# First attention: fp32 probabilities as the moving operand instead of a two-part fp16 split

## The reference, cut to what matters

```python
B, Sq, Sk, HEADS, hd = 2, 512, 1024, 16, 32       # x (2, 512, 512), ctx (2, 1024, 512)
scores = einsum('bhqd,bhkd->bhqk', qh, kh) / sqrt(hd)
causal = ki <= qi + (Sk - Sq)                      # the last 512 keys are causal
attn = softmax(where(causal, scores, -10000.0))
out = einsum('bhqk,bhkd->bhqd', attn, vh)          # keys and values are both ctx itself
```

## Time and profile before

| | us |
|---|---|
| median of 3 runs | 1868.09 (1862.59 to 1871.82) |
| span of the profiled execution, first to last instruction | 1858.6 |
| first attention in it | 234 to 571 |
| PE, DVE, ACT busy over the span | 1482.2, 1148.1, 933.8 |

### The profile page before, as it was taken

One profiled execution on the slowest core, in us unless ns is written; L12 is line 12 of the kernel. 1 busy time (PEld: TensorE's weight loads), 2 busy tenths in 40 slices (PEclk: granted clock), 3 DMA queues, 4 the chain that ended last, 5 costly groups with the idle time before them and its releaser, 6 DMA issues.

```text
span 1858.6 us, 30566 instructions
## 1 busy us (share of the span) xinstructions
PE 1482.2 (80%) x11006; PEld 830.7 (45%) x11064; DVE 1148.1 (62%) x2005; ACT 933.8 (50%) x1195; POOL 370.5 (20%) x179
## 2 busy tenths in 40 slices
PE   6885288888885299999999999277878787778777
PEld 3443155555554144444444444134545454444434
DVE  5888699899895211111111111569999999995565
ACT  3554388788783011111111111138998999892853
POOL 1101000000000366899940000320000000000150
PEclk9998599999997599999999999688999999999998
DMA  5567111121110699999988882640000000000101
GB/s 180 176 183 251 69 61 60 60 75 60 60 66 1 256 403 366 382 384 403 404 331 302 305 308 112 211 114 26 28 26 25 13 25 25 25 1 1 68 1 46
DMA packets 102757, 273.90 MB, mean 147 GB/s; under 512 B 7209, under 2 KB 11305, under 8 KB 101681
## 3 DMA queue, kind: packets, MB, share of 16 engines
q1 hardware_dynamic: 87904, 223.65, 32.4%
q0 software_dynamic: 10816, 40.90, 7.1%
q10 hardware_dynamic: 3984, 8.65, 1.2%
HBM read 212.62 MB, written 38.27 MB: 135 GB/s over the span
## 4 chain that ended last, share of the span: by engine, by line
PE 44%; DVE 34%; issue 11%; DMA 4%; ACT 3%; POOL 2%; SPq 1%; DVEq 1%; POOLq 0%; ACTq 0%
PE scores L859 17%; DVE arena L1615 15%; PE bank L875 9%; DVE arena L1420 6%; DVE arena L1434 3%; DMA arena<-in_ctx 2%; PE scores L686 2%; PE bank L773 2%; PE bank L1059 2%; PE bank L991 1%; PE bank L867 1%; DVE arena L1621 1%; PE bank L904 1%; PE bank L757 1%; PE scores L920 1%
## 5 line engine op out<-in xcount | busy, mean ns | idle before, releaser
L1615 DVE TENSOR_SCALAR_CACHE_REDUCE arena<-scores,arena 128x1024 f32<-128x1024 f32 x256 | 317.4, 1277 | 14.5 <-PE scores L920 14.3
L859 PE MATMUL scores<-arena 128*128 128x512 f32 x736 | 322.2, 596 | 0.8 <-DVE arena L1552 0.8
L1560 DVE TENSOR_TENSOR arena<-scores,arena 128x512 f32<-128x512 f32 x46 | 31.8, 692 | 447.7 <-PE scores L859 447.7
L1215 ACT ACTIVATE arena<-arena 128x2048 int16<-128x2048 f32 x128 | 256.3, 2002 | 47.9 <-DVE arena L1621 35.6
L920 PE MATMUL scores<-arena 96*128 96x512 bf16 x512 | 160.3, 400 | 88.9 <-DVE arena L1615 78.8
L859 PEld LDWEIGHTS scores<-arena 128*128 128x128 f32 x736 | 141.0, 192 | 178.0 <-issue 176.8
L875 PE MATMUL bank<-arena 128*128 128x512 f32 x368 | 163.3, 597 | 3.5 <-issue 3.3
L933 PEld LDWEIGHTS bank<-arena 128*128 128x128 bf16 x2048 | 122.8, 100 | 72.0 <-issue 68.3
L1183 ACT ACTIVATE arena<-scores 128x512 f32<-128x512 f32 x46 | 27.5, 597 | 249.1 <-PE scores L859 249.1
L933 PE MATMUL bank<-arena 128*128 128x128 bf16 x2048 | 141.5, 225 | 12.8 <-DVE arena L1640 1.7
L1150 ACT ACTIVATE arena<-bank 128x512 f32<-128x512 f32 (+3 forms) x256 | 117.8, 511 | 47.4 <-PE bank L757 36.4
(11 more groups left out here) (238 smaller groups left out, 2480.8 us busy)
## 6 DMA issues: line engine op xcount, KB each, us to landing
arena<-in_L_ffn_w SPq DMA_DIRECT2D x69, 2048.0 KB, 12.4
arena<-arena SPq DMA_DIRECT2D x64, 260.0 KB, 2.3
kst_d<-arena POOLq DMA_DIRECT2D x16, 384.0 KB, 6.4
tern_d<-arena POOLq DMA_DIRECT2D x12, 512.0 KB, 7.0
arena<-tern_d SPq DMA_DIRECT2D x3, 2048.0 KB, 10.8
arena<-kst_d SPq DMA_DIRECT2D x16, 384.0 KB, 3.5
xs_d<-arena SPq DMA_DIRECT2D x23, 256.0 KB, 3.6
arena<-xs_d SPq DMA_DIRECT2D x23, 256.0 KB, 13.2
```

Of the source, the lines that this page charges most:

```text
L859: ins = pe.matmul(scores[:, m * 1024 + half * 512:m * 1024 + half * 512 + 512], xsT[a][:, c], wa[:, m, c, half * 512:half * 512 + 512], st ...
L1215: act.activation(p16[i], ssb[i], ACT.Exp, bias=ebias[i], scale=-1.0, accum_out=rsum[a][:, t:t + 1]).then_inc(p_ready, 1)
L1615: dve.tensor_scalar(ssb[i][:, s:s + 1024], scores[:, s:s + 1024], nsq[:, bass.ds(h, 1), t], None, ALU.mult, ALU.min, accum_out=nmx[i][:, h ...
```

## The change

The values are loaded as fp32 from the context input, 32 columns, with a column of ones and 31 columns of zeros behind them: a stationary operand of 64 columns. The probabilities stay in fp32 and are the moving operand. Even key tiles give partitions 0 to 63 of `bank7`, odd ones 64 to 127, each with queries along the columns. ACT copies the bank to `oT`, and four fp32 products of `oT` with the constant `fold` (ones at row j and column j, and at row 64 + j and column j) add the two halves and turn the result back to queries by 33 columns. `p1`, `p2`, their copies and subtractions, and the sum over parts are gone. In PE's order the fold of a unit stands in the next unit behind `st` 3, and `smax` 3 comes ahead of `pv` 0.

```diff
-KROW = KBLK * HD + 2
+KROW = KBLK * HD
+VW = 64
+OW = HD + 1
+        fold = keep.take(F32, OW)
-        vst = [ra.take(BF16, KT, KROW) for _ in range(2)]
+        vst = [ra.take(F32, KT, VW) for _ in range(2)]
-        p1 = ra.take(F16, NP)
-        p2 = ra.take(F16, NP)
+        oT = ra.take(F32, SQ)
@@ SP
+            v_rows = ctx_in.rearrange("b (t p) (h d) -> b p t h d", p=P, h=H)
-                sp.dma_start(vst[a].rearrange("p t c -> p (t c)"), k_rows[:, bass.ds(u, 1)].rearrange("p u c -> p (u c)")).then_inc(v_in[a], 16)
+                sp.dma_start(vst[a][:, :, 0:HD], v_rows[bass.ds(u // H, 1), :, :, bass.ds(u % H, 1)].rearrange("b p t h d -> p (b t) (h d)")).then_inc(v_in[a], 16)
@@ POOL
+            made(pool.memset(fold, 0.0))
+            for j in range(2):
+                made(pool.affine_select(out=fold, in_=fold, compare_op=ALU.not_equal, fill=1.0, base=-VW * j,
+                                        pattern=[[-1, OW]], channel_multiplier=1))
-            pool.memset(kvrow[:, :, :, :, KBLK * HD:KROW].rearrange("p b h t c -> p (b h t) c"), 1.0).then_inc(ones_set, 1)
             for a in range(2):
                 pool.memset(kC[a][K2:K2 + 2, :], 1.0).then_inc(ones_set, 1)
+                pool.memset(vst[a][:, :, HD:OW], 1.0).then_inc(ones_set, 1)
+                pool.memset(vst[a][:, :, OW:VW], 0.0).then_inc(ones_set, 1)
...
@@ PE
             def pv(u, a, k, r, first):
                 if k == 0:
                     pe.wait_ge(v_in[a], 16 * (r + 1))
                     if not first:
-                        pe.wait_ge(oread_done, 2 * u)
+                        pe.wait_ge(o_step, 2 * u)
-                if k % 2 == 0:
-                    pe.wait_ge(p2_done, 4 * u + k // 2 + 1)
-                    pe.wait_ge(p1_done, 4 * u + k // 2 + 1)
-                for t in range(max(0, k - HALF), QT):
-                    c = OFF[k] + (t * P - (SQ - WID[k]))
-                    for part in (p1, p2):
-                        ins = pe.matmul(bank7[:, t * 97:t * 97 + 97], part[:, c:c + P], vst[a][:, k, HD:HD + 97], ...)
+                pe.wait_ge(exp_done, KT * u + k + 1)
+                w, row = WID[k], VW * (k % 2)
+                ins = pe.matmul(bank7[row:row + VW, SQ - w:SQ], vst[a][:, k], eP[:, OFF[k]:OFF[k] + w],
+                                start=k < 2, stop=k >= KT - 2, skip_group_check=True)
+            def fold_out(u):
+                pe.wait_ge(oT_made, at(u))
+                for t in range(QT):
+                    ins = pe.matmul(bank7[:, t * OW:(t + 1) * OW], oT[:, t * P:(t + 1) * P], fold, start=True, stop=True)
+                ins.then_inc(o_folded, 1)
@@ PE att_unit
                 st(u, a, 2, first); st(u, a, 3, first)
+                if not first:
+                    fold_out(u - 1)
                 if not last:
                     smax(u + 1, b, 2)
                 st(u, a, 4, first); st(u, a, 5, first)
-                pv(u, a, 0, r, first); pv(u, a, 1, r, first)
                 if not last:
                     smax(u + 1, b, 3)
+                pv(u, a, 0, r, first); pv(u, a, 1, r, first)
@@ ACT
+            def copy_oT(u, first):
+                act.wait_ge(pv_done, 4 * u + 4)
+                if not first:
+                    act.wait_ge(o_folded, at(u - 1))
+                act.activation(oT, bank7[:, :], ACT.Copy).then_inc(oT_made, 1)
...
-                    act.activation(p1[:, s:e], eP[:, s:e], ACT.Copy).then_inc(p1_done, 1)
+                    if j == 1 and not first:
+                        copy_oT(u - 1, not past(u, 2))
@@ DVE
-            def rest_of_p(u, g):
-                dve.tensor_tensor(p2[:, s:e], eP[:, s:e], p1[:, s:e], ALU.subtract).then_inc(p2_done, 1)
-                dve.tensor_reduce(osum, bank7[:, 0:4 * 97]..., X, ALU.add).then_inc(oread_done, 1)
+            def finish_unit(u):
+                folded = bank7[:, 0:QT * OW].rearrange("p (t c) -> p t c", t=QT)
+                dve.wait_ge(o_folded, at(u))
+                dve.reciprocal(rl, bank7[:, HD:QT * OW:OW]).then_inc(o_step, 1)
+                dve.wait_ge(o_step, 2 * u + 1)
+                dve.tensor_tensor(oatt..., folded[:, :, 0:HD], each(rl, [QT, HD]), ALU.mult).then_inc(o_step, 1)
```

More of the change, by code:

```diff
@@ L64 @@
 LN_EPS, RMS_EPS = 1e-5, 1e-6
-CONSTS = 13
+CONSTS = 16
 LN_STEPS = 3 * NT + 6
@@ L233, in program @@
         eP = ra.take(F32, NP)
-        p1 = ra.take(F16, NP)
-        p2 = ra.take(F16, NP)
+        oT = ra.take(F32, SQ)
         mx = ra.take(F32, QT)
         mparts = ra.take(BF16, QT, 2)
-        osum = ra.take(F32, QT, HD)
         rl = ra.take(F32, QT)
@@ L348, in program @@
         smax_done, max_done, m_step = sem("smax_done"), sem("max_done"), sem("m_step")
-        st_done, exp_done, p1_done, p2_done = (sem(n) for n in ("st_done", "exp_done", "p1_done", "p2_done"))
-        pv_done, oread_done, o_done = (sem(n) for n in ("pv_done", "oread_done", "o_done"))
+        st_done, exp_done = sem("st_done"), sem("exp_done")
+        pv_done, oT_made, o_folded, o_step = (sem(n) for n in ("pv_done", "oT_made", "o_folded", "o_step"))
         att_added = sem("att_added")
@@ L561, in _ @@
                 pool.memset(kC[a][K2:K2 + 2, :], 1.0).then_inc(ones_set, 1)
+                pool.wait_ge(ones_set, 3 * a + 1)
+                pool.memset(vst[a][:, :, HD:OW], 1.0).then_inc(ones_set, 1)
+                pool.wait_ge(ones_set, 3 * a + 2)
+                pool.memset(vst[a][:, :, OW:VW], 0.0).then_inc(ones_set, 1)
+                pool.wait_ge(ones_set, 3 * a + 3)
             pool.wait_ge(r_step, R_STEPS)
@@ L765, in pv @@
                     if not first:
-                        pe.wait_ge(oread_done, 2 * u)
-                if k % 2 == 0:
-                    pe.wait_ge(p2_done, 4 * u + k // 2 + 1)
-                    pe.wait_ge(p1_done, 4 * u + k // 2 + 1)
-                for t in range(max(0, k - HALF), QT):
-                    c = OFF[k] + (t * P - (SQ - WID[k]))
-                    for part in (p1, p2):
-                        ins = pe.matmul(bank7[:, t * 97:t * 97 + 97], part[:, c:c + P], vst[a][:, k, HD:HD + 97],
-                                        start=(k == 0 and t == 0 and part is p1), stop=(k == KT - 1 and t == QT - 1 and part is p2),
-                                        skip_group_check=True)
+                        pe.wait_ge(o_step, 2 * u)
[3 more added lines that the diff above has]
+                                start=k < 2, stop=k >= KT - 2, skip_group_check=True)
                 if k % 2:
                     ins.then_inc(pv_done, 1)
+            def fold_out(u):
[3 more added lines that the diff above has]
+                ins.then_inc(o_folded, 1)
             def att_unit(u, a, r, first, last):
@@ L799, in att_unit @@
                     st(u + 1, b, 0, False); st(u + 1, b, 1, False)
-                pv(u, a, 4, r, first); pv(u, a, 5, r, first)
-                pv(u, a, 6, r, first); pv(u, a, 7, r, first)
+                for k in range(4, KT):
+                    pv(u, a, k, r, first)
+                if last:
+                    fold_out(u)
             turn_keys(0, 0, 0)
@@ L805, in _ @@
             pe.wait_ge(vf_done, NC)
-            pe.wait_ge(ones_set, 3)
+            pe.wait_ge(ones_set, 6)
             for t in range(QT):
@@ L818, in _ @@
             pe.wait_ge(exp_done, UNITS * KT)
-            pe.wait_ge(oread_done, 2 * UNITS)
+            pe.wait_ge(o_step, 2 * UNITS)
             for c in range(KC):
@@ L1091, in kv_tile @@
                 act.wait_ge(ctx_loaded[a], 16 * (k + 1))
-                if first:
-                    act.wait_ge(ones_set, 1)
                 parts = context_parts(u)
@@ L1141, in copy_m @@
                 act.activation(qC[b][K2:K2 + 2, :], scores[:, 0:512].bitcast(BF16)[K2:K2 + 2, 0:SQ], ACT.Copy).then_inc(m_ready, 1)
+            def copy_oT(u, first):
[3 more added lines that the diff above has]
+                act.activation(oT, bank7[:, :], ACT.Copy).then_inc(oT_made, 1)
             def att_unit(u, a, k, first, last):
                 b = 1 - a
[L1145 to L1154, removed]
-                    act.activation(p1[:, s:e], eP[:, s:e], ACT.Copy).then_inc(p1_done, 1)
+                for j in range(KT):
+                    if j % 2 == 0 and not first:
+                        act.wait_ge(pv_done, 4 * (u - 1) + j // 2 + 1)
+                    act.wait_ge(st_done, KT * u + j + 1)
+                    act.activation(eP[:, OFF[j]:OFF[j] + WID[j]], (bank4, bank5)[j % 2][:, 0:WID[j]], ACT.Exp, scale=SCALE).then_inc(exp_done, 1)
+                    if j == 1 and not first:
+                        copy_oT(u - 1, not past(u, 2))
                 if within(u + 2, UNITS):
@@ L1159, in att_unit @@
                     copy_m(u + 1, b)
+                if last:
+                    copy_oT(u, False)
             act.preload_act_table(ACT.Exp)
@@ L1429, in split_m @@
                 dve.scalar_tensor_tensor(mparts[:, :, 1], mx, -1.0, mparts[:, :, 0], ALU.mult, ALU.subtract).then_inc(m_step, 1)
```

(22 more changed lines are left out.)

## The result

The changed kernel takes 1872.42 us (median of 20 runs) against 1864.09 of the kernel before (20 runs beside it): ratio 1.0042, 95% interval 1.0026 to 1.0058. A second comparison gave 1.0037 (1.0020 to 1.0054). So it is slower, by 8 us; I had forecast 29. Two kernels further down each had one slow run of six, which their medians and ratios leave out.

What follows compares the result with a forecast made beforehand. DVE, in a ring with PE, bounds the first attention; after the change PE alone: 6.08 + 3.87 + 0.97 + 0.54 + 0.2 = 11.66 us a unit against 10.76, so 1897 us; range 1875 to 1912, overall 1850 to 1955.

Steps and rivals of the forecast that it cites:

- The new products: PE's fp32 products of values and probabilities: 3.87 us a unit, between 2.99 (full overlap) and 5.58 (none).
- the stepping: Records A, A' (even tile), B, B' (odd) start in order; only B runs beside A': 1.29 us a 512-column pair.
- my lower bound: New products on PE with each odd tile wholly beside its even one: 2.99 us a unit.
- The fold: Four fp32 PE calls, eight records at 0.121 us each: 0.97 us a unit, bounds 0.5 to 1.4.
- The change of shape: PE entering and leaving the 64-column stationary three times a unit: 6 x 0.09 = 0.54 us, bounds 0 and 1.2.
- The wait for the copied maximum: Next unit's first score product on PE waits for ACT's copy of the maximum: 0.2 us a unit.
- The sum: PE's terms in a unit of the first attention: 11.66 us against 10.76, +0.90 us.
- Neither can hold a unit of 10 us any more: DVE falling to 5.1 us and ACT to 5.7 us a unit, so PE decides alone.
- The keys behind the 128-byte pieces: Next keys, queued behind the new value load, might come 0.1 to 2.4 us late; counted as nothing.
- Faster by more: Outcome of the whole kernel: faster by more than about 0.5% (9 us), chance 0.22.
- rival 1: Both column tiles of the new products overlap fully, 2.99 us a unit: 1853 to 1870 us; chance 0.30.
- wrong if the period is under 10.7; then the pairs overlap fully: Sign against the forecast: first-attention unit period under 10.7 us would mean pairs of new products overlap fully.

Runs made afterwards that it cites:

- one-tile kernel: Changed kernel with even and odd key tiles both in partitions 0 to 63 of the bank, so one column tile; period 13.54 us, 1949.6 us (one run).
- full-width kernel: As the one-tile kernel, but the values padded to 128 stationary columns; period 13.02 us, 1935.2 us (one run).
- extra load: Changed kernel plus four DVE subtractions a unit on constant data, at the old places of the removed ones; period 11.76 us, ratio 1.0125.
- order 4, 6, 5, 7: Changed kernel with the last four products (key tiles 4 to 7) reordered so calls of one column tile are neighbours; period 10.98 us, 1869.8 us.
- both with transposes: Changed kernel with the four fold products replaced by four fp32 transposes and DVE adding the halves; period 10.60 us, ratio 0.9980.
- fastest kernel: Changed kernel with transposes for the fold, key tiles 0 to 3 in one run, last four products ahead of next unit's first scores; 1839.7 us, ratio 0.9865.

## Why the prediction was wrong

The bound moves from DVE to PE, as forecast; the size is wrong, 29 us against 8, and so is the step behind it. The sign came right in part by luck: with the overlap that came, the prediction's own terms give 10.78 us a unit, +2 us in all, no change that could be told. That it is 8 comes from borders and a wait that were sized 0.34 us too small together, less a fold sized 0.16 too large. Step by step:

- **The new products: the step that failed.** I took 3.87 us a unit, from the stepping, in which B stands behind A'. In the trace the records of the two tiles do not wait for each other: B starts 0.006 us after A (400.221 and 400.227), and the one-tile kernel prices the second tile at 2.56 us, which is full overlap. What I called half of the array shows in the runs as the form of the records, 128*64 against the 128*128 of a full-width call, and as the 0.43 to 0.48 us between the starts of two 512-column records of one tile. So my lower bound, 3.00 us, was the price. The 0.87 us are 27 us over the stage, more than the whole error of 21. The row from which I argued, that PE's records start in the program's order, was never tested there: in this stage of the kernel before no two neighbouring calls lie in different column tiles.
- **The fold** was sized 0.97 and cost 0.81, shown by leaving it out. 5 us too many. The row gave 14 records in 1.70 us from the first start to the last end, the last one's tail included; start to start they are 0.11 us apart, there with 8 columns and in the fold with 33, and the fold's first two only 0.03.
- **The change of shape** was sized 0.54. The six changes cost 0.09 to 0.10 each, 0.56, under the 0.16 us tail that my upper bound had put on each. Besides, in each run the second record of a tile starts 0.48 us after the first, not 0.43, which I had not counted: 0.15 a unit. The full-width kernel has it too, so it is not the shape. Together 0.72 us (0.15 + 0.15 + 0.14 behind the runs, 1.01 - 0.86 twice and 1.43 - 1.29, and 0.09 ahead of each).
- **The wait for the copied maximum** was counted as 0.2, as the bracket of the row said. Start to start PE loses 0.36 there: the last transpose of line 729 starts at 404.08, the next call could follow at 404.13 and starts at 404.49, since the bracket begins only where the last records' tails end (404.30); the exit from a 64-column form is part of it. 0.16 too few.
- **The sum** with the measured terms: 6.08 + 3.00 + 0.81 + 0.72 + 0.36 = 10.97 us; measured 10.98. The 6.08 was a busy time; start to start what stays is 6.07 in the changed kernel, so it served here. PE's time added up, so the method was sound; the product was the one term far off.
- **"Neither can hold a unit of 10 us any more"** was right for the changed kernel, but the argument does not carry. I judged DVE by its busy time. The extra load shows that DVE can stay at 9.4 us a unit and still cost 0.78 by standing ahead of what PE waits for.
- **The keys behind the 128-byte pieces** were not late. The new load lands in 2.4 us where I had bounded it by 6.4, the last issue line here:

```profile
arena<-in_ctx SPq DMA_DIRECT2D x32, 128.0 KB, 2.4
```

- **The chances, the range and the sign of being wrong** did not follow from the terms. "Faster by more" had 0.22, mostly from rival 1, though with my own 0.09 us a change full overlap is +2 us. The bounds of fold and shape add up to 1866 to 1931, not to 1875 to 1912. And "wrong if the period is under 10.7; then the pairs overlap fully" would have missed it: the pairs overlap fully at 10.98.

Rival 1 named the mechanism that came, at 10.78 with the change of shape; I gave it 0.30 and the stepping 0.38.

The order of starts and the order of signals are two things in these runs. The starts did not keep the program's order: with the order 4, 6, 5, 7 call 5 began beside call 4 (417.31 and 417.30 us). The signals did: that of call 5 came 0.03 us behind the end of call 6, the last call that stands ahead (418.83 and 418.80).

## What to carry to other kernels

When an engine loses half of its work, add up the next one start to start before anything else: here PE had 1.9 us of room in a unit (10.76 less 8.83 busy), and 0.25 for the new products over the old, 0.81 for the fold, 0.72 for the borders of the runs and 0.36 for a wait took more than that. Fuse runs of one tile shape, but look first at what each piece was covering: eight in one run lost 0.48 us (11.46 against 10.98), four in one run gained 0.17 (10.43 against 10.60, both with transposes). And when a row's rule comes from code that never tests it, as the order of starts did here, carry both ends at near equal chance.

## What the runs showed of the hardware that I had not expected

- Two fp32 calls in different column tiles (64 columns at 0, 64 at 64) ran fully beside each other: four records of 512 columns in 1.08 us in the changed kernel, 1.93 in the one-tile kernel.
- A call of one column tile started past records of the other tile that stand ahead of it, over one and a half calls with the order 4, 6, 5, 7 (417.31 against 417.78 to 418.42; period unchanged at 10.98 us). The semaphores still changed in program order: in the changed kernel that of call 7 0.03 us behind the end of call 6 (31 units of 31), with the order 4, 6, 5, 7 that of call 5 as much behind it.
- It was seen past bf16 records too. In the fastest kernel the first product of the upper tile (384 columns, call 5) starts at 417.20, before the last of the four bf16 transposes with 64 columns and before call 4 (512 columns), which both stand ahead of it; so in 30 of 32 units:

```profile
417.06 0.35 PE L730 MATMUL bank<-arena 128*64 128x128 bf16 x3
417.20 0.54 PE L781 MATMUL bank<-arena 128*64 128x384 f32 x1
417.25 0.22 PE L730 MATMUL bank<-arena 128*64 128x128 bf16 x1
417.31 1.46 PE L781 MATMUL bank<-arena 128*64 128x512 f32 x7
```
